# The turn between two halves of a fused attention and FFN kernel: one batch's row statistics, its weighing, the last scale split and GpSimd's additions change place

## The reference, cut to what matters

```
x = x + xattn(layernorm(x), ctx)            # 8 heads, softmax, projection Wo, bias bo
h = layernorm(x, ln1_g, ln1_b)
h = bitlinear(h, w1, b1)                    # 256 -> 1024
h = gelu(h)
h = layernorm(h, ln2_g, ln2_b)
h = bitlinear(h, w2, b2)                    # 1024 -> 256
x = x + h

bitlinear(x, w, b):   sx = 127 / max(|row of x|);   sw = 1 / mean(|w|)
    (clip(round(x * sx), -128, 127) / sx) @ (clip(round(w * sw), -1, 1) / sw) + b
```

## Time and profile before

| | |
|---|---|
| median of 3 runs | 1031.87 us (1030.28 to 1032.79) |
| the profiled execution | 1029.65 us, of which the span from the first to the last instruction 1028.0 us |
| busy share of the span: TensorE, VectorE | 90%, 89% |
| ScalarE, GpSimd | 91%, 75% |
| mean granted clock of TensorE | 0.979 of full speed |

### The profile page before, as it was taken

How to read it: one execution, slowest core, us unless ns; L and a number is a source line. 1 busy time by engine, 2 the same in 40 slices (tenths; PEclk the granted TensorE clock), 3 DMA queues, 4 the chain that set the end, 5 groups by cost and what they waited for, 6 DMA issues and landing times.

```text
span 1028.0 us, 26021 instructions
## 1 busy us (share of the span) xinstructions
PE 925.0 (90%) x7442; PEld 557.9 (54%) x7442; DVE 915.9 (89%) x1202; ACT 930.3 (91%) x2659; POOL 772.3 (75%) x1182
## 2 busy tenths in 40 slices
PE   6999999999999999999999767888888888888886
PEld 4666666666666666666666413344444444444435
DVE  2688888888888888888888899999999999999996
ACT  4789999999999999999997868999999999999993
POOL 3266666777666666666667667999999999999997
PEclk9999999999999999999999967999999999999998
DMA  5589967786686666565665315877777777777787
GB/s 173 147 156 201 191 171 157 172 168 167 146 180 170 164 162 165 164 172 168 154 165 128 104 45 90 124 123 122 123 123 121 123 122 122 122 122 122 122 124 122
DMA packets 276079, 146.98 MB, mean 143 GB/s; under 512 B 183320, under 2 KB 266520, under 8 KB 276016
## 3 DMA queue, kind: packets, MB, share of 16 engines
q1 hardware_dynamic: 258432, 129.29, 56.9%
q0 software_dynamic: 16864, 16.26, 13.2%
q10 hardware_dynamic: 720, 0.66, 0.2%
HBM read 71.62 MB, written 33.63 MB: 102 GB/s over the span
## 4 chain that ended last, share of the span: by engine, by line
PE 54%; DVE 24%; issue 11%; ACT 5%; POOL 4%; DVEq 1%; DMA 1%; ACTq 0%; POOLq 0%
PE banks L1379 12%; PE banks L1370 10%; DVE g_max L864 9%; PE banks L1291 6%; PE banks L1343 6%; DVE gn_low L852 5%; DVE gn_high L852 5%; PE banks L1332 5%; PE banks L1363 4%; PE banks L1353 3%; PE banks L1321 2%; PE banks L1357 2%; POOL nq L595 2%; PE banks L1259 1%; DVE gn_high L838 1%
## 5 line engine op out<-in xcount | busy, mean ns | idle before, releaser
L1225 PE MATMUL banks<-w_t,h_t 128*128 128x512 bf16 x504 | 136.6, 395 | 75.5 <-DVE gn_low L838 39.1
L1082 ACT ACTIVATE banks<-banks,h_dq 128x1024 f32<-128x1024 f32 x128 | 141.9, 1109 | 13.0 <-PE banks L1230 11.1
L754 DVE TRANSPOSE_TENSOR_REDUCE nm_part<-banks 128x64 f16<-128x2048 f32 x64 | 147.6, 2306 | 2.6 <-PE banks L1291 2.2
L1088 ACT ACTIVATE g_dev<-banks,g_sum 128x1024 bf16<-128x1024 f32 x128 | 146.2, 1142 | 0.0
L1035 ACT ACTIVATE probs<-banks 120x512 f32<-120x512 f32 x256 | 132.2, 602 | 14.4 <-PE banks L1321 10.9
L1259 PE MATMUL banks<-w_t,g_t 128*128 128x256 bf16 x1024 | 135.9, 277 | 5.4 <-ACT h L1121 4.7
L1379 PE MATMUL banks<-wo_sb,o_t 128*128 128x256 f32 x512 | 136.4, 402 | 4.1 <-DVE o_t L774 3.7
L1225 PEld LDWEIGHTS banks<-w_t,h_t 128*128 (+1 forms) x504 | 47.9, 99 | 137.0 <-issue 102.6
L1259 PEld LDWEIGHTS banks<-w_t,g_t 128*128 128x128 f16 x1024 | 92.5, 99 | 54.3 <-issue 38.6
L1370 PE MATMUL banks<-xt,wq_c 128*128 128x256 f32 x512 | 121.3, 380 | 0.0
L537 POOL COPY h_dq<-h_cl 128x2 f32<-128x2 f32 (+1 forms) x64 | 11.9, 187 | 143.1 <-DVE h_qs L817 138.2
(11 more groups left out here) (168 smaller groups left out, 2523.1 us busy)
## 6 DMA issues: line engine op xcount, KB each, us to landing
x_in<-in_x SPq DMA_DIRECT2D x64, 256.0 KB, 4.8
xt<-in_x_t SPq DMA_DIRECT2D x64, 256.0 KB, 4.1
xr<-in_x SPq DMA_DIRECT2D x64, 256.0 KB, 4.3
out<-xr SPq DMA_DIRECT2D x64, 256.0 KB, 6.5
out<-h POOLq DMA_DIRECT2D x62, 256.0 KB, 5.0
ctx_t<-in_ctx_t SPq DMA_DIRECT2D x64, 128.0 KB, 3.9
r_bc<-r_rows SPq DMA_DIRECT2D x63, 128.0 KB, 4.1
w_raw<-in_w_t SPq DMA_DIRECT2D x8, 256.0 KB
```

Source lines behind the costliest of these rows:

```text
L754: dve.tensor_reduce(nm_part[:, :, 0:C * RB], blocks_p, AX.X, ALU.max, negate=True, apply_transpose=True).then_inc(max_done, 1)
L1082: act.activation(u_p[t], u_p[t], ACT.Gelu, scale=h_dq[:, b, t:t + 1], accum_out=g_sum[:, p, t:t + 1]).then_inc(gelu_done, 1)
L1088: act.activation(g_dev[:, t, :], u_p[t], ACT.Square, scale=-float(F), bias=g_sum[:, p, t:t + 1], accum_out=g_ssq[:, p, t:t + 1]).then_inc( ...
L1225: pe.matmul(u_p[t][:, cols], h_t[:, b, t * C + c, :], w1_t[:, c, cols], start=(c == 0), stop=False, skip_group_check=True)
```

## The change

On VectorE, `weigh(63)` moves ahead of `affine_h(61)`; `statistics(63)` goes, and `centre_h(63)` takes its means from ScalarE; `add_y(63)` and the centres of batch 0 move; `split_last` goes, and `invert_scales(2)` moves behind step 4 of the second half. On ScalarE, a new `last_statistics` stands between `ffn(0)` and `ffn(1)`, and the casts of batches 60, 61 and 63 change place. On GpSimd, `scale_last` replaces batch 63's `power`, `add_b2` of the batches 60 to 63 moves behind other work, and the last split is made by `split_scales(2)` and `split_rest(2)` behind steps 4 and 5, where the wait for the stores of x1 now stands too. SP's wait for those stores goes to the end of its list. TensorE waits for batch 62's `add_y` ahead of `project(63)`, and for the last turned rows and the split only behind step 7.

```
 SP:
                 steps(sp, A0, NB + 5, L0, L1, attn, 4, aside)
-                for r in range(4):
-                    sp.wait_ge(x1_stored[r], NB * 4)
...
                 sp.wait_ge(last_stored, 16 * 2 * T)
+                for r in range(4):
+                    sp.wait_ge(x1_stored[r], NB * 4)
 GpSimd:
+                def scale_last(m):
+                    pool.wait_ge(x1_ssq, (NB - 2) * T + T)
+                    pool.tensor_tensor(f_ve[:, m, :], f_ssq[:, m, :], var_mul[:, :], ALU.mult).then_inc(f_ve_done, 1)
+                    pool.wait_ge(f_ve_done, 2 * (NB - 2) + 1)
+                    pool.tensor_tensor(f_ve[:, m, :], f_ve[:, m, :], var_add[:, :], ALU.add).then_inc(f_ve_done, 1)
+                    pool.wait_ge(f_ve_done, 2 * (NB - 2) + 2)
+                    pool.wait_ge(h_affine, NB - 2)
+                    pool.tensor_tensor(f_r[:, m, :], f_ve[:, m, :], neg_half[:, 0:T], ALU.pow).then_inc(f_r_done, 1)
...
                 quantise(NB - 3, 1)
+                gain_part(0, 0, 0)
+                power(NB - 2, 2)
                 add_b2(NB - 4, 0)
-                power(NB - 2, 2)
-                pool.wait_ge(h_centred, NB - 1)
+                gain_part(0, 1, 0)
+                first_scales(0)
+                scale_last(1)
+                quantise(NB - 2, 2)
                 add_b2(NB - 3, 1)
-                gain_part(0, 0, 0)
-                quantise(NB - 2, 2)
-                first_scales(0)
-                gain_part(0, 1, 0)
+                gain_part(1, 0, 1)
+                gain_part(1, 1, 1)
+                first_scales(1)
                 add_b2(NB - 2, 2)
-                gain_part(1, 0, 1)
-                power(NB - 1, 3)
-                add_b2(NB - 1, 3)
-                first_scales(1)
-                gain_part(1, 1, 1)
                 gain_part(2, 0, 2)
                 quantise(NB - 1, 3)
+                add_b2(NB - 1, 3)
                 scales(2, 0)
                 gain_part(2, 1, 2)
                 quantise_batch(0, 0)
-                for r in range(4):
-                    pool.wait_ge(x1_stored[r], NB * 4)
                 ffn(3, 3)
-                steps(pool, 4, NB, FFN_L0, FFN_L1, ffn, 4)
+
+                def first_parts_stored():
+                    split_rest(2)
+                    for r in range(4):
+                        pool.wait_ge(x1_stored[r], NB * 4)
+
+                steps(pool, 4, NB, FFN_L0, FFN_L1, ffn, 4, {4: lambda: split_scales(2), 5: first_parts_stored})
 VectorE:
-                def split_last():
...
                 centre_h(NB - 3, 1, [f_mean[:, 1, t:t + 1] for t in range(T)])
+                weigh(NB - 1, 1)
                 affine_h(NB - 3, 1)
                 add_y(NB - 2, 2)
                 statistics(NB - 2, 2)
-                centre_h(NB - 2, 2, [f_mv[:, 0, t, 0:1] for t in range(T)])
-                weigh(NB - 1, 1)
                 dve.wait_ge(gains_loaded, 32)
                 centre(0, 0, 0)
+                add_y(NB - 1, 3)
+                centre_h(NB - 2, 2, [f_mv[:, 0, t, 0:1] for t in range(T)])
+                centre(0, 1, 0)
                 affine_h(NB - 2, 2)
-                add_y(NB - 1, 3)
-                centre(0, 1, 0)
-                statistics(NB - 1, 3)
-                centre_h(NB - 1, 3, [f_mv[:, 1, t, 0:1] for t in range(T)])
+                dve.wait_ge(x1_ssq, (NB - 2) * T + T)
+                centre_h(NB - 1, 3, [f_mean[:, 1, t:t + 1] for t in range(T)])
                 ffn(1, 1)
                 affine_h(NB - 1, 3)
                 ffn(2, 2)
                 ffn(3, 3)
-                invert_scales(2)
-                split_last()
-                steps(dve, 4, NB, FFN_L0, FFN_L1, ffn, 4)
+                steps(dve, 4, NB, FFN_L0, FFN_L1, ffn, 4, {4: lambda: invert_scales(2)})
 ScalarE:
+                def last_statistics(p, r):
+                    act.wait_ge(f_ve_done, 2 * (NB - 2))
+                    act.wait_ge(h_centred, NB - 2)
+                    act.wait_ge(x1_done, NB)
+                    for t in range(T):
+                        act.activation(g_dev[:, t, 0:D], xr[:, r, t, :], ACT.Copy, scale=1.0 / D,
+                                       accum_out=f_mean[:, p, t:t + 1]).then_inc(x1_summed, 1)
+                    for t in range(T):
+                        act.wait_ge(x1_summed, (NB - 2) * T + t + 1)
+                        act.activation(g_dev[:, t, 0:D], xr[:, r, t, :], ACT.Square, scale=-1.0,
+                                       bias=f_mean[:, p, t:t + 1], accum_out=f_ssq[:, p, t:t + 1]).then_inc(x1_ssq, 1)
...
                 ffn(0, 0)
+                last_statistics(1, 3)
+                ffn(1, 1)
                 cast_rows(NB - 4, 0)
                 cast_rows(NB - 3, 1)
-                ffn(1, 1)
                 cast_rows(NB - 2, 2)
                 ffn(2, 2)
+                cast_rows(NB - 1, 3)
                 ffn(3, 3)
-                cast_rows(NB - 1, 3)
-                act.wait_ge(x1_done, NB)
 TensorE:
                 turn_bias(2)
+                pe.wait_ge(x1_done, NB - 1)
                 project(NB - 1, 1)
...
-                for r in range(4):
-                    pe.wait_ge(turned[r], NB * 4)
-                pe.wait_ge(last_split, 5)
-                steps(pe, 4, NB, FFN_L0, FFN_L1, ffn, 4)
+
+                def all_rows():
+                    for r in range(4):
+                        pe.wait_ge(turned[r], NB * 4)
+                    pe.wait_ge(split_chain, 15)
+
+                steps(pe, 4, NB, FFN_L0, FFN_L1, ffn, 4, {FFN_L0 - 1: all_rows})
```

More of the change, by code:

```diff
@@ L247, in xattn_ffn @@
         split_chain = sem("split_chain")
-        last_split = sem("last_split")
         bt_ps = sem("bt_ps")
@@ L633, in ffn @@
                     quantise_batch(j - 2, (n + 2) % 4)
+                def scale_last(m):
[6 more added lines that the diff above has]
+                    pool.tensor_tensor(f_r[:, m, :], f_ve[:, m, :], neg_half[:, 0:T], ALU.pow).then_inc(f_r_done, 1)
                 def power(b, m):
                     pool.wait_ge(h_affine, b - 1)
-                    pool.wait_ge(last_ve, b - NB + 3)
+                    pool.wait_ge(last_ve, 1)
                     pool.tensor_tensor(f_r[:, m % 2, :], f_ve[:, m % 2, :], neg_half[:, 0:T], ALU.pow).then_inc(f_r_done, 1)
@@ L878, in statistics @@
                     last.then_inc(x1_stats, 1)
-                    dve.wait_ge(x1_stats, b - NB + 3)
+                    dve.wait_ge(x1_stats, 1)
                     for t in range(T):
@@ L882, in statistics @@
                     last.then_inc(x1_aggr, 1)
-                    dve.wait_ge(x1_aggr, b - NB + 3)
+                    dve.wait_ge(x1_aggr, 1)
                     dve.tensor_scalar(f_ve[:, p, :], f_mv[:, p, :, 1], 1.0 + LN_EPS, LN_EPS * LN_EPS,
@@ L1217, in rows_up @@
                         pe.wait_ge(bt_done, b + 2 - n % 2)
-                        if isinstance(b, int) and b < 6:
+                        if isinstance(b, int) and b <= FFN_L0:
                             pe.wait_ge(turned[n], 16 * (b // 4) + 16)
```

## The result

The changed kernel took 1027.80 us (median of 7 runs, 1026.84 to 1028.55) where the kernel before took 1032.54 (7 runs, 1030.28 to 1035.29): ratio 0.995, 95% interval 0.9927 to 0.9972. The time lies inside the predicted range; the gain between the medians, 4.7 us, is larger than the 2.9 us forecast. The two profiled executions differ by less than the medians: 1027.94 against 1029.65 us, 1.7 us.

What follows compares the result with a forecast made beforehand. VectorE bounds the FFN loop, so only centre(5, 0)'s start, closing the attention-to-FFN turn, was thought to matter: 2.9 us earlier, from 1029.65 to 1026.75 profiled, from 1031.87 to 1029.0 by the median. Range 1025.3 to 1031.6 us.

Steps and rivals of the forecast that it cites:

- rival (a): GpSimd's additions mostly slip in beside centre, add_y and largest on VectorE: 4 to 5.6 us gained; chance 0.23.
- The weighing and project(63): Weighing ahead delays affine_h(61) by 0.26 us; TensorE starts project(63) at 586.18 instead of 588.91 and takes 1.99 us.
- The statistics: Batch 63's statistics move to ScalarE: VectorE loses some 2 us of work, ScalarE gains 1.9 us inside a wait.
- The additions: GpSimd's b2 additions hold up VectorE: 0.9 us at centre_h(62), 1.25 at affine(0), 1.1 at affine(1); centre(2, 1) at 609.0.
- its bound: Upper bound if no addition met VectorE: centre(5, 0) near 625.4, 5.6 us earlier.
- The short powers: GpSimd's short powers do not stop VectorE, charged nothing; by the skill's rule batch 63's power would cost 0.7 us.
- The inversion: VectorE's invert_scales(2), 0.6 us, costs nothing behind largest(3), as centre(5, 0) waits there anyway; without that cover, 0.6.
- ScalarE late next: With the split gone, VectorE waits 0.8 us for ScalarE's part(4, 0); centre(4, 0) comes 2.8 us earlier.
- that instruction: centre(5, 0), where VectorE enters the gapless loop: 628.1 instead of 631.01, 2.9 us earlier, all carried to the end.
- Rival (b): Statistics' gain returns as lost turns and low-clock project(63), split's as ScalarE's lateness in steps 4 and 5: 0 to 1.5 us; chance 0.22.
- rival (c): GpSimd becomes the bound, scales(2) late for affine(2): slower, 1034 to 1037 us; chance 0.07.

Runs made afterwards that it cites:

- a_stat_back: Changed kernel with batch 63's statistics back on VectorE and its power on GpSimd; centre(3, 0) 1.30 us later, centre(6, 0) 1.55 later; no timed ratio given.
- a_no_adds: Changed kernel with GpSimd's b2 additions for batches 60 to 63 cut from 256 columns to 2 a tile; centre(6, 0) at 50.81 us, no timed ratio given.
- a_adds_late: Changed kernel with the b2 additions of batches 60 to 63 moved to steps 4 (two), 5 and 6; 1025.44 us, ratio 0.9935 to before.
- b_split: Kernel before with only the last split on GpSimd behind steps 4 and 5 and the inversion behind step 4; timed ratio 1.0034.
- a_split_back: Changed kernel with the last split and the inversion back on VectorE between steps 3 and 4; timed ratio 0.9971.
- before_copy: The kernel before, unchanged, timed against itself on another chip; ratio 0.9998 (0.9970 to 1.0026).
- after_again: The changed kernel, unaltered, run again on another chip against the kernel before; ratio 0.9963 (0.9935 to 0.9991).
- a_late_fill: a_adds_late plus 4 to 24 unused matmuls behind the rows up of steps 0 to 4, fitted to the waits; 1024.68 us, ratio 0.9931 to before.

## Why the prediction was right, and where it was off

The time fell inside the range and the list of the turn came out nearly as laid out. That the median fell there is in part luck: it lies where rival (a) put it (1026.3 to 1027.9), whose mechanism did not happen, while the first pair of profiles gained 2.1 us, less than the 2.9 forecast, and the medians 4.7, more. Point by point:

The weighing and project(63): affine_h(61) started 0.27 us later (0.26 forecast), project(63) at 585.99 (586.18) and took 1.99 us. Right.

The statistics: ScalarE's eight instructions took 1.9 us (589.11 to 591.01), as forecast, in its hole. a_stat_back shows their worth to VectorE, 1.30 us at centre(3, 0), and in that kernel no addition met L881.

The additions: centre_h(62) took 1.74 us in place of 0.87 (0.9 lost as forecast), affine(0) 2.26 and 1.74 (1.4 lost, 1.25 forecast), the second half of affine(1) 2.28 (1.0, forecast 1.1). centre(2, 1) came at 608.39 where 609.0 was forecast. That it is the additions is shown by a_no_adds and a_adds_late. Rival (a) is out for this kernel, and its bound was 0.6 us short: without the additions centre(5, 0) came 6.2 us earlier than before (44.09 against 50.26), where 5.6 was the bound.

The short powers: batch 63's power, 0.82 us at 591.90, fell on affine_h(62), which kept 0.86; 0.7 us were not lost. The rule of the Trainium skill (SBUF — State Buffer, section "SBUF: two separate sides"), by which the engine that loses the shared port stops for the whole instruction of the other, is not borne out by this row, as it was not by that of the prediction: the power began 0.26 us before affine_h(62) ended, and neither lost much (0.82 us, where the power at 587.36 took 0.70). The measurement decides. GpSimd's rounding, on the other hand, did hold up a small instruction: L740, from 625.97, took 1.12 us, about as long as the second half of L594 beside it (625.93 to 627.05), where L729 had taken 0.23. The inversion was costed at nothing; it used up the cover, for centre(5, 0) followed it at once.

ScalarE late next: centre(4, 0) waited 0.68 us for `part` (0.8 forecast) and came 3.5 us earlier (2.8). centre(5, 0) came 3.5 us earlier (2.9).

The step that failed stands in the first paragraph: "Whatever makes that instruction earlier makes the end earlier by as much, since loop and tail are untouched." Between centre(5, 0) and the loop lies the second tile of step 5, and in the first profile of before TensorE's clock was back for it (granted 0.91 in the stretch 630 to 632). The work moved forward by 3.5 us, the rise of the clock did not, and the same tile cost rows up of 2.9 and rows down of 2.1 us: centre(5, 1) waited 1.30 us. So 3.5 us became 2.1 in the pair of profiles: a small error (0.6 us too cautious) against a larger one (1.4 us given back). b_split and a_split_back show the same wait of 1.30 us, before_copy shows it in the kernel before, after_again less of it, and a_late_fill removes its cause.

Reading the granted clock in slices of 1 us shows that the place of its rise goes with this wait in all twelve profiles without added matmuls. Where the clock was back 0.1 to 1.0 us ahead of centre(5, 0) (the first three of before, a_no_adds), centre(5, 1) did not wait; where it came back 0.2 us behind it (after_again), centre(5, 1) waited 0.28 us; where 3.8 us or more behind it (the other seven), 1.30. So the loss belongs to a pair of executions and not to the change as such: with the clock late in both, the changed kernel keeps its 3.5 us at centre(6, 0) (54.67 against the 58.21 of before_copy). Whether the change itself moves the rise, these few profiles do not show.

Rival (b), that the split's gain comes back as ScalarE's lateness, was right for the split alone, measured against the first profile of before; rival (c) did not happen: scales(2) was done at 609.35 and affine(2) began at 612.45.

What stays open: the medians differ by 4.7 us and the two profiles by 1.7. The place of the clock's rise accounts for up to 4.6 between two executions, but whether the timed runs had that mix, or differed ahead of the turn, was not seen, as they have no trace.

## What to carry to other kernels

Before a saving is carried to the end of a program, look past the instruction where it arises to the first stretch without a wait, and ask which of the waits in between belong to an engine whose speed changes: gains of 1.6 and 3.5 us in front of a half-clocked TensorE ended as 0.2 and 2.1 against an execution whose clock was back earlier, and as 1.7 and 3.5 against one with a late clock too. An addition on GpSimd, 1.27 us long, cost VectorE up to 1.0 us here when both read two SBUF tensors, so its place among the other engine's instructions is part of its price; moved to steps where VectorE's second operand lies in PSUM, the four lengthened none of its instructions, though in a_late_fill GpSimd then came late with a scale. Work that nobody reads can shorten a turn, if it is fitted to the waits: in one profile each, 94 matmuls took 4.1 us out of this one up to centre(6, 0), 2.5 up to centre(20, 0), and a coarse helping of 80 left no such gain. That it pays in the timed runs is not shown.

## What was not expected of the hardware

The clock of TensorE did not follow the program's steps. In the kernel before it rose 49 to 50 us behind centre_h(61) in three profiles and 54 in a fourth, in the changed kernel 51 and 47, each time with the same instructions ahead of it, and in a_adds_late TensorE was busy for all of 10 us (620 to 630) at 0.50 before it rose. Up to centre(5, 0) the turn otherwise repeated within 0.1 us on every chip seen (0.3 at centre(1, 0)), while the first half ended anywhere between 580 and 613 us.
